# Reordering the start of a fused conditioned-residual kernel: transposes of block 0 before the class product, l1 of block 1 before the row product, other counts of products of ones

## What is computed

```python
x = x + L0(x)   # U = (cond @ W_dec + b).reshape(B, 257, 30); x @ (U @ V) + bias
x = x + L1(x)   # style = cond @ aff.T/sqrt(128) + b; y = (x*style) @ W.T * dcoef; clip(y + bias)
x = x + L2(x)   # relu(x @ (down*dg + db)) @ (up*ug + ub) + x
x = x + L3(x)   # the six parts below
h = ln(ln(x)*pw_g[id] + pw_b[id]) * cp_g[c] + cp_b[c]
t = ln(x)*tm_g[c] + tm_b[c];  s = ln(x)*ms_g[m] + ms_b[m]
m, n, r = x + mlp_ln(memory), x + mlp_ln(noise), x + mlp_ln(resource)
cat = concat([w0*h, w1*t, w2*m, w3*n, w4*r, w5*s])     # w = softmax(aw)
L3 = ln(silu(cat @ W1 + b1) @ W2 + b2) * g + be
```

## Time and profile before

| what | value |
|---|---|
| median of 3 runs (lowest, highest) | 536.58 us (534.08, 537.15) |
| the profiled execution | 537.51 us |
| its span, first to last instruction | 535.7 us |
| mean granted TensorE clock | 0.981 |
| TensorE matmul busy | 499.5 us, 93% |
| VectorE, ScalarE, GpSimd busy | 76%, 61%, 73% |

### The profile page before, as it was taken

How to read it: one execution, slowest core, us unless ns; L and a number is a source line. 1 busy time by engine, 2 the same in 40 slices (tenths; PEclk the granted TensorE clock), 3 DMA queues, 4 the chain that set the end, 5 groups by cost and what they waited for, 6 DMA issues and landing times.

```text
span 535.7 us, 9958 instructions
## 1 busy us (share of the span) xinstructions
PE 499.5 (93%) x3450; PEld 353.1 (66%) x3450; DVE 406.2 (76%) x707; ACT 326.7 (61%) x622; POOL 390.3 (73%) x365
## 2 busy tenths in 40 slices
PE   2987989899999999999999999999999999999993
PEld 2953635576767676767676767767676767677682
DVE  1949685857878797878787878878787978887753
ACT  4583557444767576667574756657576757655822
POOL 6568598779796978777877877787868693787321
PEclk9999798899999999999999999999999999999998
DMA  8887641424515080807161524335261614104102
GB/s 298 241 305 208 175 98 41 119 60 120 142 56 146 17 223 1 230 9 206 34 183 56 161 79 120 120 71 169 48 193 41 189 34 99 47 8 153 39 2 78
DMA packets 35622, 61.85 MB, mean 115 GB/s; under 512 B 5985, under 2 KB 18045, under 8 KB 35212
## 3 DMA queue, kind: packets, MB, share of 16 engines
q1 hardware_dynamic: 29532, 44.16, 29.6%
q0 software_dynamic: 5344, 16.87, 10.9%
q10 hardware_dynamic: 720, 0.48, 0.3%
HBM read 52.63 MB, written 8.87 MB: 115 GB/s over the span
## 4 chain that ended last, share of the span: by engine, by line
PE 78%; DVE 9%; DMA 4%; issue 4%; ACT 2%; SPq 1%; DVEq 0%; POOL 0%; POOLq 0%; ACTq 0%
PE ps_c L906 13%; PE ps_c L908 11%; PE ps_c L907 11%; PE ps_d L952 9%; PE ps_a L982 6%; PE ps_d L966 5%; PE ps_a L1000 3%; PE ps_a L994 3%; DVE tm_t_l L1434 3%; PE ps_b L939 3%; PE ps_b L1000 3%; DMA set_wdec<-in_nets_rows 2%; PE ps_b L923 2%; DMA set_wdec<-in_W_dec 1%; PE ps_a L488 1%
## 5 line engine op out<-in xcount | busy, mean ns | idle before, releaser
L1499 POOL DMA_INDIRECT pw_rows<-in_pw,gidx x64 | 63.6, 994 | 17.8 <-issue 17.7
L952 PE MATMUL ps_d<-xm_t,l_w 128*128 128x512 f32 x128 | 59.0, 603 | 1.1 <-POOL xm_t L1508 1.1
L1208 ACT ACTIVATE h<-h,nb_h,rstd_h 128x256 f32<-128x256 f32 x64 | 33.3, 593 | 34.6 <-POOL nb_h L1523 34.6
L1508 POOL TENSOR_TENSOR xm_t<-x_t,style 128x1024 f32<-128x1024 f32 x16 | 30.5, 1906 | 30.5 <-DVE x_t L1338 29.7
L1538 POOL TENSOR_TENSOR h<-xhat,pw_rows 128x1024 f32<-128x1024 f32 x16 | 38.0, 2372 | 9.3 <-ACT xhat L1208 7.1
L952 PEld LDWEIGHTS ps_d<-xm_t,l_w 128*128 128x128 f32 x128 | 23.1, 190 | 25.8 <-issue 24.6
L1557 POOL TENSOR_TENSOR w_up<-up_rep,ugub 128x1024 f32<-128x1024 f32 x16 | 37.9, 2371 | 2.2 <-issue 2.0
L1543 POOL TENSOR_TENSOR h<-h,pw_rows 128x1024 f32<-128x1024 f32 x16 | 38.3, 2391 | 1.3
L1559 POOL TENSOR_TENSOR w_up<-w_up,ugub 128x1024 f32<-128x1024 f32 x16 | 38.2, 2390 | 1.3
L1267 ACT ACTIVATE h_t_h<-ps_b 128x1024 fp32r<-128x1024 f32 x16 | 16.4, 1028 | 36.5 <-PE ps_b L1000 36.5
L906 PE MATMUL ps_b<-w_h,act_t_l 128*128 128x256 f32 x128 | 37.7, 295 | 0.4 <-DVE act_t_l L1447 0.4
(11 more groups left out here) (245 smaller groups left out, 1544.7 us busy)
## 6 DMA issues: line engine op xcount, KB each, us to landing
ugub<-ugub_scratch SPq DMA_DIRECT2D x32, 512.0 KB
x_t<-in_x_t SPq DMA_DIRECT2D x16, 512.0 KB
out<-y_out SPq DMA_DIRECT2D x15, 512.0 KB
set_wdec<-in_W_dec SPq DMA_DIRECT2D x2, 1920.0 KB, 9.8
set_wdec<-in_int_W SPq DMA_DIRECT2D x1, 1536.0 KB, 10.0
set_wdec<-in_nets_rows SPq DMA_DIRECT2D x1, 1152.0 KB
pw_rows<-in_pw,gidx POOLq DMA_INDIRECT x64
set_wdec<-in_nets_W SPq DMA_DIRECT2D x1, 768.0 KB, 5.7
```

The source lines that it names most:

```text
L952: m = eng.matmul(ps_l1[:, o, :], l1_w[:, k, o * P:(o + 1) * P], xm_t[:, k, :], start=k == 0, stop=k == KB - 1)
L1208: m = eng.activation(out[:, j, :], src[:, j, :], ACT.Identity, bias=nb[k][:, j:j + 1], scale=rstd[k][:, j:j + 1])
L1499: eng.indirect_dma_start(pw_rows[c.ring][:, j, :], None, t["pw"], bass.IndirectOffsetOnAxis(ap=gidx[c.ring][:, j:j + 1], axis=0)).then_inc ...
```

## The change

Only the `begin` lists and the counts of `pe_warm` change. The loop and the end are the same on every engine. The VectorE list is untouched.

```diff
-            s, v, out, count = ((c_ug, 1, ps_d[:, 0, :], 13), (v_dca, 1, ps_a[:, 0, :], 13),
-                                (v_x1, 2, ps_b[:, 0, :], 7), (v_x1, 2, ps_b[:, 0, :], 9))[c.n]
+            s, v, out, count = ((c_ug, 1, ps_d[:, 0, :], 13), (v_dca, 1, ps_a[:, 0, :], 18),
+                                (v_dca, 1, ps_a[:, 0, :], 5), (v_x1, 2, ps_b[:, 0, :], 4))[c.n]
...
-                             (pe_cls, 0), (pe_x3r, 0), (pe_row, 0), (pe_l1, 1), (pe_xht, 0), (pe_t, 2),
-                             (pe_warm, 2), (pe_dn, 1), (pe_cp, 0), (pe_warm, 3), (pe_up, 1), (pe_x1, 2),
+                             (pe_x3r, 0), (pe_cls, 0), (pe_l1, 1), (pe_xht, 0), (pe_row, 0), (pe_t, 2), (pe_dn, 1),
+                             (pe_cp, 0), (pe_warm, 3), (pe_up, 1), (pe_x1, 2), (pe_x3r, 1), (pe_t, 3), (pe_l1, 2),
```

More of the change, by code:

```diff
@@ L1588, in _ @@
                              (load_ids, 0), (load_up, 0), (load_x, 2), (load_ids, 1), (load_ub, 2), (load_up, 1),
-                             (load_ub, 3), (load_x, 3), (load_ub, 4), (load_ids, 2), (load_up, 2), (load_ub, 5),
-                             (load_x, 4), (load_shift, 0), (load_shift, 1), (load_up, 3), (load_up, 4),
-                             (load_x, 5), (load_ids, 3), (load_shift, 2), (load_up, 5)],
+                             (load_ub, 3), (load_x, 3), (load_ub, 4), (load_ids, 2), (load_up, 2), (load_shift, 0), (load_shift, 1), (load_ub, 5), (load_x, 4),
+                             (load_up, 3), (load_up, 4), (load_x, 5), (load_ids, 3), (load_shift, 2), (load_up, 5)],
                       order=[(load_ids, 2), (load_shift, 3), (load_x, 0), (load_ub, 0), (load_up, 0), (store, 6)],
@@ L1606, in _ @@
                              (pe_ug, 0), (pe_t, 0), (pe_dc, 0), (pe_hid, 0), (pe_x1, 0), (pe_warm, 0), (pe_mo, 0),
-                             (pe_l1, 0), (pe_t, 1), (pe_warm, 1), (pe_dn, 0), (pe_mot, 0), (pe_up, 0), (pe_x1, 1),
-                             (pe_cls, 0), (pe_x3r, 0), (pe_row, 0), (pe_l1, 1), (pe_xht, 0), (pe_t, 2),
-                             (pe_warm, 2), (pe_dn, 1), (pe_cp, 0), (pe_warm, 3), (pe_up, 1), (pe_x1, 2),
-                             (pe_x3r, 1), (pe_t, 3), (pe_l1, 2), (pe_shift, 0), (pe_w1_x3, 0), (pe_tm, 0),
-                             (pe_hht, 0), (pe_dn, 2), (pe_ms, 0)],
+                             (pe_l1, 0), (pe_t, 1), (pe_warm, 1), (pe_dn, 0), (pe_warm, 2), (pe_mot, 0), (pe_up, 0), (pe_x1, 1),
+                             (pe_x3r, 0), (pe_cls, 0), (pe_l1, 1), (pe_xht, 0), (pe_row, 0), (pe_t, 2), (pe_dn, 1),
+                             (pe_cp, 0), (pe_warm, 3), (pe_up, 1), (pe_x1, 2), (pe_x3r, 1), (pe_t, 3), (pe_l1, 2),
+                             (pe_shift, 0), (pe_w1_x3, 0), (pe_tm, 0), (pe_hht, 0), (pe_dn, 2), (pe_ms, 0)],
                       order=[(pe_xht, 5), (pe_w1_tm, 6), (pe_up, 4), (pe_w1_ms, 6), (pe_cp, 5), (pe_x1, 3),
@@ L1639, in _ @@
                              (act_gidx, 1), (act_th2, 1), (act_relu, 0), (act_mot, 0), (act_w1high, 0), (act_u, 2),
-                             (act_onehot, 0), (act_x3, 0), (act_x3h, 0), (act_xnorm, 0), (act_shift, 0),
-                             (act_th1, 2), (act_th2, 2), (act_xht, 0), (act_rowwrite, 0), (act_relu, 1),
+                             (act_onehot, 0), (act_x3h, 0), (act_x3, 0), (act_xnorm, 0), (act_xht, 0),
+                             (act_shift, 0), (act_th1, 2), (act_th2, 2), (act_rowwrite, 0), (act_relu, 1),
                              (act_gidx, 2), (act_gidx, 3), (act_u, 3), (act_hnorm, 0), (act_onehot, 1), (act_u, 4),
@@ L1707, in _ @@
                       begin=[(g_init, 0), (g_b2rows, 0), (g_dcoef, 0), (g_style, 0), (g_gather, 0), (g_moroot, 0),
[L1708 to L1711, removed]
+                             (g_wup, 0), (g_gather, 1), (g_style, 1), (g_rootx, 0), (g_wup, 1), (g_hmul, 0), (g_hadd, 0),
+                             (g_res, 0), (g_rooth, 0), (g_w1xlow, 0), (g_w1tlow, 0), (g_w2low, 0), (g_style, 2),
+                             (g_w1mlow, 0), (g_rootx, 1), (g_wup, 2), (g_hmul, 1), (g_hadd, 1), (g_gather, 2),
+                             (g_rooth, 1), (g_res, 1), (g_style, 3), (g_gather, 3), (g_rootx, 2)],
                       order=[(g_wup, 3), (g_hmul, 4), (g_hadd, 4), (g_rooty, 6), (g_gather, 2), (g_rooth, 4),
```

## The result

| | before | changed |
|---|---|---|
| median of 20 runs | 535.72 us | 538.08 us |
| lowest, highest | 530.85, 541.78 us | 535.06, 542.71 us |
| profiled execution, its span | 537.51, 535.7 us | 538.36, 536.5 us |

The ratio is 1.005, with a 95% interval of 1.0026 to 1.0074. The changed kernel is slower by half a per cent. The forecast was 0.4 us less than before.

A forecast was written before the change was run, and what follows sets the result against it. TensorE, busy 93%, was taken as the bound, with only the start able to move the time. Terms -2.7 + 1.3 - 0.74 + 1.8 = -0.34 gave 537.1 us profiled, 536.2 from the median; range 533.3 to 538.9.

The forecast's parts named there:

- What bounds: Whole kernel: TensorE bounds it, busy 93%; the untouched loop changes the time only by when TensorE reaches it.
- Early ones: Extra products of ones before `pe_dn` of block 0 and L544: fit inside idles, cost nothing, keep the clock up, gain nothing.
- The step at T: Block 0 transposes before class product, row product later: `pe_l1` of block 1 ends at 67.15, not 69.84; gain 2.7 us.
- T: Mark on the way to the loop: end of `pe_l1` of block 1, 69.84 us before, forecast 67.15.
- From T to L: Later L843 on GpSimd delays `g_style` and so `pe_l1` of block 2: 19.9 us instead of 18.63, loss 1.3 us.
- L: Mark on the way to the loop: start of `pe_l1` of block 2, 88.47 us before.
- Shift rows: Before L1078 (`pe_shift`), behind `pe_l1` of block 2: rows loaded sooner, so the wait for memory goes; gain 0.74 us.
- The clock at L: TensorE idles 3 to 5.6 us before `pe_l1` of block 2, which starts at half clock; loss 1.8, bounds 0.5 and 3.6.
- The sum: Whole kernel: -2.7 + 1.3 - 0.74 + 1.8 = -0.34, say 0.4 us less; chance 0.57.
- The rivals: Whole kernel, three other outcomes: full clock 533.8 us (0.18), nothing arrives 536.6 (0.14), slower 540.8 (0.11).
- The slower one: Class product and `pe_l1` of block 2 at half clock throughout after the new idles: +4.2, 540.8 us; chance 0.11.

The follow-up runs named there:

- second trace: The kernel before, unchanged, run and profiled again as its own control: 532.38 us, ratio 0.9971; profiled span 529.0 us.
- the filled version: Changed kernel with L843 at its old place and products of ones in four TensorE idles: 528.55 us, ratio 0.9882; repeated 530.21 us, ratio 0.9909.
- 15 ones: Changed kernel plus 15 products of ones before `pe_l1` of block 2, L843 left late: 537.49 us, ratio 1.0058 to before.
- both: Changed kernel with L843 at its old place and 8 products of ones before `pe_l1` of block 2: 535.15 us, ratio 0.9999 to before.
- L843 back: Changed kernel with one move undone, L843 (`g_w1tlow`) ahead of `g_style` of block 1 again: 533.03 us, ratio 0.9994 to before.

## Why the prediction was wrong

**What bounds, and that the loop passes the start on.** Right. Traces that differ by 7 us at L1014 need 402.7 us from there; the five with a stretch at half near 500 us need 1.5 more.

**Early ones.** Right that they cost nothing and delay nobody: `pe_up` of block 0 starts 5.07 us behind the end of `v_x2add` (L1360) in both kernels (48.72 and 48.31). In the changed kernel `pe_up` of block 0 and its surroundings ran at full clock to 55 us, and nobody was sooner for it.

**The step at T.** This is the step that failed: transposes first, row product later, priced as a gain of 2.7 us. The value for the changed kernel was right within 0.8 us (67.9 for 67.15). The gain was taken as the difference to 69.84, the mark of one execution of before in which the clock was at half from 54 to 61 us, as if before always met that stretch. Counted from the start of `pe_up` of block 0, the end of `pe_l1` of block 1 lies at these distances:

| | at full clock | with a stretch at half near 55 us |
|---|---|---|
| old order | 12.8 | 16.05 |
| new order | 12.3 | 14.6 |

The old order's 12.8 is from its second trace and 16.05 from its first, whose `pe_up` is this row:

```profile
53.79 3.17 PE L982 MATMUL ps_a<-act_dn,w_up 64*128 64x64 f32 x32 [0.72 <-ACT act_dn L1188]
```

The new order's 12.3 is from the filled version (52.93 to 65.26), where the ones end before the transposes can start. So the new order gains 1.5 us where both meet half clock, 0.5 where neither does, and loses 1.8 where only it does. The prediction had only the first of these cases. The means suggest that the last one counts: the changed kernel loses 12.1 us to the clock and before 9.5, and the class product put first again takes it to 8.1. Why the new order meets half clock more often is not shown. In its profile, and in two of its variants (15 ones, both), the clock fell 1.1 to 1.6 us before the new idle began; in two others (L843 back, and transposes first on before) it fell 0.3 to 0.4 us behind the idle's end.

**From T to L.** The mechanism was right: 86.97 - 67.94 = 19.0 against 19.9, L843 in the place and with the effect described, 2.36 us long and not 2.88 (the prediction's 2.54 was the nearer value). But the old L was again taken from the slow start: at full clock it is 83.67, or T + 17.0, not T + 18.6. So the loss in this step is 2.0 us, not 1.3.

**Shift rows.** The wait went, as said. In the quick execution of before it isn't there either (87.28, right behind `pe_l1`), so it was worth less than 0.74 on the whole.

**The clock at L.** The mechanism was right, the size was off: 6.73 - 3.69 = 3.0 us for the 1.8 taken, near the upper bound of 3.6. The stretch at half lasted from 86.3 to 93.1 us. This is the largest miss inside the pair of traces, 1.2 us.

**The sum.** For the two profiled executions it is -1.9 + 0.4 - 0.74 + 3.0 = +0.8 (T, T to L, wait, clock), and the spans differ by 0.8. So as a difference of two traces it was off by 1.1 us, and it came that near because misses of 0.8 (T), 0.9 (T to L) and 1.2 us (clock at L) went against each other in part. The other 1.6 us of the miss are the step from the traces to the medians. The profiled execution of before lies 1.8 us above its own median of 20, that of the changed kernel 0.3 above. The clock explains this in part only: before's profile splits into 525.5 + 10.2, its mean into 523.6 + 9.5, so most of the excess is time at full clock. Of the 3.2 us between the means of the two kernels, 2.6 are in the part lost to the clock and 0.6 in the rest.

**The rivals.** The slower one named the right kind of loss, a low clock at both places, though the first stretch began before its idle. It was given a chance of 0.11 because I measured it against a trace that already had the same stretch. The advice of the Trainium skill ("TensorE: Matmul & The Clock Gate", Part 1) to leave the ramp out of a model would have led further off: 534.5 us for the 538.08 measured. The runs here disagree with it: the clock took 9.5 of before's 533 us, 1.8%, and 2.6 of the 3.2 us between the kernels are in its part.

What is not settled: how the loss divides between the swap and L843. Each alone adds to before 1.4 and 1.7 us of span x clock and leaves no quick execution (the swap with the row product still ahead of `pe_l1`), and undoing either in the changed kernel brings three of them back; together they don't add up to the sum of both. The moves on ScalarE and SyncE were not tried alone.

## What to carry to other kernels

An idle of TensorE can cost more than itself: the 4.4 us here were followed by 3 us lost at half clock. It need not: behind the idle of 1.5 to 1.8 us before `pe_cp` the clock fell in six of eleven profiles. Before a reordering is priced from one trace, ask which of its stretches at half clock the old order always has and which this execution happened to have, and take the marks of both orders at the same clock; the mean clock of each timed execution shows how often either occurs. Filling one idle did not lower the lost part beyond its error (10.8 and 12.1 against the changed kernel's 12.1, 11.0 against 10.2 with L843 back); filling four brought it to 3.8. Size the filling by the later work's release, since too much of it is waited for. When an experiment undoes one move of several, check what the others leave standing in its way: the swap on the kernel before was not the swap of the changed one.

## What the runs showed of the hardware

The same program, on the same inputs, had its start (to 96 us) at full clock in one profile and three stretches at half in the other. Its times lie in two clusters that go with the mean clock: in the first set of 35 runs seven from 529.1 to 530.2 us, all at 0.991 or 0.992, the others from 532.9 to 539.1, all at 0.985 or less.

Idles of the same length were followed by a fall or not. TensorE stood idle for 1.47 to 1.84 us before `pe_cp` of block 0 in eleven profiles, and the clock fell within 2.2 us behind it in six. Behind the idle of 1.85 us before L1014 of block 0 it fell in nine of the same eleven. A fall came also without an idle straight ahead of it: in the kernel with seven ones before the transposes the granted clock was 0.59 in the microsecond from 57 us, where TensorE had run `pe_up` and `pe_x1` of block 0 and then ones without a pause since 54.2.

L843 took 2.88 us in the trace of before, where it started at 56.54 us and VectorE's gain table (L673, both inputs in SBUF) ran until 57.2. At its late place it took 2.36 and 2.38. At its old place in the second execution of before it started behind the gain table, and took 2.40:

```profile
57.32 2.40 POOL L843 TENSOR_TENSOR w_l<-set_wdec,w_h 128x1024 fp32r<-128x1024 f32 x1
```

The Trainium skill, "SBUF — State Buffer", in its section on SBUF's two separate sides, gives a lock between a GpSimd instruction that reads SBUF and a VectorE one with two SBUF inputs. These numbers agree with it.
